# First attention: VectorE's operations in another order, weighing one step later, centring on ScalarE

## The reference, cut to what matters

```
q, k, v = x @ Wq.T + bq, x @ Wk.T + bk, x @ Wv.T + bv      # 16, 8, 8 heads of 16
q, k = rotated by position (cos, sin)
p = (x / max(|x|, 1e-6)) @ R.T           # for q and k, 8 features a head
feats = concat(sin(p), cos(p)) / 4
kv  = einsum('bhsf,bhsd->bsfd', kp, v)   # sums over the heads
out = einsum('bhsf,bsfd->bhsd', qp, kv)
```

## Time and profile before

| | us |
|---|---|
| median of 3 runs | 2040.08 (2039.08 to 2040.45) |
| profiled execution, its own time | 2036.14 |
| its span | 2034.0 |
| busy: PE, DVE, ACT, POOL | 1682.5, 1383.6, 939.3, 672.0 |
| mean granted TensorE clock | 0.923 |

### The profile page before, as it was taken

How to read it: one execution, slowest core, us unless ns; L and a number is a source line. 1 busy time by engine, 2 the same in 40 slices (tenths; PEclk the granted TensorE clock), 3 DMA queues, 4 the chain that set the end, 5 groups by cost and what they waited for, 6 DMA issues and landing times. The chain is left out here.

```text
span 2034.0 us, 35680 instructions
## 1 busy us (share of the span) xinstructions
PE 1682.5 (83%) x10296; PEld 1295.6 (64%) x10296; DVE 1383.6 (68%) x2825; ACT 939.3 (46%) x2201; POOL 672.0 (33%) x850
## 2 busy tenths in 40 slices
PE   2899985709991780799999999996789999979997
PEld 2787774509991560455555555542579999968886
DVE  5688887506665876977777777760467777646776
ACT  0456562304443651066666666664444444433343
POOL 1555530750007824043434334343000000047760
PEclk9799998959995995899999999998899999989999
DMA  6445523723434996333535354422774444466661
GB/s 217 181 141 168 156 47 65 230 91 117 125 113 127 332 355 190 85 105 86 147 85 144 94 129 109 118 68 64 205 216 125 125 126 125 127 212 182 202 181 47
DMA packets 288529, 293.13 MB, mean 144 GB/s; under 512 B 122665, under 2 KB 245034, under 8 KB 286300
## 3 DMA queue, kind: packets, MB, share of 16 engines
q1 hardware_dynamic: 265340, 236.62, 39.6%
q0 software_dynamic: 18432, 50.36, 7.9%
q10 hardware_dynamic: 4608, 4.20, 0.6%
HBM read 144.97 MB, written 141.82 MB: 141 GB/s over the span
## 5 line engine op out<-in xcount | busy, mean ns | idle before, releaser
L1705 ACT ACTIVATE ca_PT<-ca_psS 128x512 f32<-128x512 f32 (+3 forms) x768 | 344.9, 493 | 272.8 <-PE ca_psS L1740 260.4
L1631 DVE TENSOR_REDUCE ca_part<-ca_psM 128x1 f32<-128x512 f32 (+3 forms) x608 | 368.6, 657 | 85.3 <-PE ca_psM L1725 60.5
L1740 PE MATMUL ca_psS<-ca_QS,ca_KS 128*128 128x512 f32 (+3 forms) x768 | 305.7, 408 | 4.2 <-ACT ca_PT L1705 4.1
L1033 POOL DMA_INDIRECT g_y<-ys_scratch,pos x128 | 129.6, 1013 | 441.7 <-POOLq L68 395.0
L1718 PE MATMUL ca_psM<-ca_KS,ca_QS 126*128 126x512 f32 (+3 forms) x768 | 246.5, 364 | 15.6 <-issue 12.8
L1740 PEld LDWEIGHTS ca_psS<-ca_QS,ca_KS 128*128 128x128 f32 x768 | 147.1, 194 | 106.7 <-ACT ca_PT L1705 101.7
L1718 PEld LDWEIGHTS ca_psM<-ca_KS,ca_QS 126*128 126x128 f32 x768 | 141.1, 193 | 37.9 <-DVE ca_part L1631 15.6
L1752 PE MATMUL ca_psO<-ca_PT,ca_VA 128*32 128x512 f32 (+3 forms) x1536 | 160.7, 497 | 1.3 <-POOL ca_PT L1611 1.3
L1609 POOL TENSOR_TENSOR ca_waited<-ca_waited 1x1 f32<-1x1 f32 x128 | 23.4, 183 | 341.7 <-ACT ca_PT L1705 341.7
L626 POOL DMA_INDIRECT xs_scratch<-x_sb,pos x128 | 123.3, 964 | 36.8 <-issue 36.8
L497 PE MATMUL fa_psO<-fa_weighed,ident 128*128 128x256 f32 x512 | 124.0, 398 | 8.1 <-DVE fa_weighed L356 8.0
(11 more groups left out here) (288 smaller groups left out, 4567.2 us busy)
## 6 DMA issues: line engine op xcount, KB each, us to landing
f_xs<-xs_scratch SPq DMA_DIRECT2D x214, 128.0 KB, 2.1
ys_scratch<-f_ys SPq DMA_DIRECT2D x214, 128.0 KB, 1.7
xs_scratch<-fa_blank SPq DMA_DIRECT2D x32, 640.0 KB, 4.1
ca_QS<-qk_scratch SPq DMA_DIRECT2D x32, 512.0 KB, 6.6
ca_KS<-qk_scratch SPq DMA_DIRECT2D x32, 512.0 KB, 8.2
xs_scratch<-fa_blank SPq DMA_DIRECT2D x32, 384.0 KB, 3.4
f_raw<-in_ffn SPq DMA_DIRECT2D x16, 608.0 KB, 4.0
v_scratch<-gp_v_st SPq DMA_DIRECT2D x32, 256.0 KB, 4.5
```

The lines of the kernel that those rows point to most:

```text
L1033: pool.indirect_dma_start(dst[:, k, :], None, y_dram, bass.IndirectOffsetOnAxis(pos[:, tile, k:k + 1], 0)).then_inc(got, 16)
L1631: dve.tensor_reduce(dst, psM[(slot * NU + u) % SLOTS][:, 0:nh * w].rearrange("p (h k) -> p h k", h=nh), AX.X, ALU.max)\
L1705: act.activation(PT[:, s % 2, h, off:CHUNK], psS[(GH * s + h) % SLOTS][:, off:CHUNK], ACT.Exp)\
L1740: pe.matmul(psS[tile % SLOTS][:, off:CHUNK], KS[:, slot, h, kt * P:(kt + 1) * P], QS[:, slot, h, c * CHUNK + off:(c + 1) * CHUNK], start=T ...
```

## The change

VectorE's list is put in another order, with normalise first; the centring moves from VectorE to ScalarE, where it is an activation with a bias of -4 from a new tile; weigh goes from lag 10 to 11, sum_groups from 11 to 12, take_out from 12 to 13, store from 13 to 14. A third memset fills the bias tile, and SP, TensorE and ScalarE wait for it.

```diff
-            in_steps(sp, (0, empty), (1, keep), (13, store), first=16)
+            in_steps(sp, (0, empty), (1, keep), (14, store), first=16)
...
-            def centre(t, i, b):
-                dve.wait_ge(A_done, t + 1)
-                dve.tensor_scalar(A[:, i % 2, :, :], A[:, i % 2, :, :], RF / 2.0, None, ALU.subtract).then_inc(centred, 1)
...
-            in_steps(dve, (1, low_half), (4, bounded_norm), (10, sine_sums), (4, inverse_norm), (0, normalise), (7, in_turns),
-                     (10, centre), (7, whole_turns), (10, weigh), (7, fraction), (2, square_norm), (8, differences), first=16)
+            in_steps(dve, (0, normalise), (1, low_half), (2, square_norm), (11, weigh), (4, bounded_norm), (4, inverse_norm),
+                     (7, in_turns), (7, whole_turns), (7, fraction), (10, sine_sums), (8, differences), first=16)
...
+            def centre(t, i, b):
+                act.wait_ge(A_done, t + 1)
+                act.activation(A[:, i % 2, :, :], A[:, i % 2, :, :], ACT.Identity, bias=minus[:, 0:1]).then_inc(centred, 1)
...
-            in_steps(act, (0, high_half), (1, take_qkv), (9, sines), (1, take_v), (1, keep_logits), (2, keep_rotT), (12, take_out),
-                     (9, squares), (3, keep_p), (3, norm), first=16)
+            act.wait_ge(ones_done, 3)
+            in_steps(act, (11, centre), (0, high_half), (1, take_qkv), (9, sines), (1, take_v), (1, keep_logits), (2, keep_rotT),
+                     (13, take_out), (9, squares), (3, keep_p), (3, norm), first=16)
...
+            pool.memset(minus[:, :], -RF / 2.0).then_inc(ones_done, 1)
...
-            in_steps(pe, (1, project), (0, transpose), (2, transpose_rotated), (11, sum_groups), (3, random_projection), first=16)
+            in_steps(pe, (1, project), (0, transpose), (2, transpose_rotated), (12, sum_groups), (3, random_projection), first=16)
```

More of the change, by code:

```diff
@@ L245, in first_attention @@
         out = sb("out", [P, 2, NQ])
+        minus = sb("minus", [P, 1])
         blank = sb("blank", [P, EMPTY[1] * HID])
@@ L258, in _ @@
         def _(sp):
-            sp.wait_ge(ones_done, 2)
+            sp.wait_ge(ones_done, 3)
             def keep(t, i, b):
@@ L489, in _ @@
             pe.wait_ge(bias_part, 4)
-            pe.wait_ge(ones_done, 2)
+            pe.wait_ge(ones_done, 3)
             def sum_groups(t, i, b):
```

## The result

The changed kernel took 2068.13 us in the median (2060.66 to 2075.55), the kernel before 2040.07; the ratio is 1.014, 95% interval 1.0102 to 1.0177. Run again beside the experiments it took 2063.47 against 2040.3: 1.0101 (1.0058 to 1.0144). Slower, as forecast, but by 23 to 28 us, not 7, and outside the range.

The account below looks back on a forecast made before the run. TensorE and VectorE, both about nine tenths busy, bound the first attention; four groups 5.0, fifth fourth step 0.8, tail 1.0 and last centring 0.1 gave +6.9 us: 2043.0 profiled, 2047.0 on the median's scale, range 2033 to 2056.

Parts of the forecast that it names:

- the stall moves from bounded_norm to weigh: VectorE, every fourth step: idle time sits before weigh, released by ScalarE's centring, some 1.5 to 2.1 us.
- TensorE no longer waits for normalise but for low_half: TensorE: waits for normalise's result are gone, and those for low_half's result are about 4 us each.
- a fourth step is 11.5 us: First attention, every fourth step: centring behind table load and root delays weigh, and low_half's result comes at 11.49 us.
- the others alternate between 7.3 and 7.9: Ordinary steps of the first attention: 7.32 us, then 7.93 when weigh waits for GpSimd's L444, in turn.
- the worked 34.06 us for four steps: Steady part: 11.49 + 7.32 + 7.93 + 7.32 us; 33.9 was taken, +1.25 on the old 32.62.
- the port conflicts between VectorE and GpSimd: Some VectorE instructions and GpSimd's exclude each other; L436 and L444 hold VectorE off 0.9 us, L441 0.5.
- the price of chained instructions: VectorE: in_turns, whole_turns, fraction in a row cost +0.18 us a step; bounded_norm and inverse_norm +0.3 every fourth step.
- Sine_sums never waits: VectorE: sine_sums needs no port and runs beside GpSimd's L436; given as a sign that the forecast is right.
- table loads rival: ScalarE: activation with bias needs loads of 1.28 us each step, about +46 us, 2086; chance 0.02.
- the next begins as the first did: Working of ordinary steps: after the 7.93 us step, the following one starts like the first, of 7.32 us.
- Much slower: Rival: ordinary steps lose 0.6 to 0.8 us to the port, each group gets a clock fall; +14, 2054 us; chance 0.19.
- The tail: End of the stage, GpSimd done, VectorE setting the pace: 8 steps costing 1.0 us, and 0.1 for the last centring.

Follow-up runs that it names:

- with the clock kept up: The changed kernel plus 16 unread 128x128 matmuls at the end of TensorE's step in every fourth step: 2042.76 us, ratio 1.0021 to the kernel before.
- later turns: Kernel before, with bounded_norm and inverse_norm at the end of VectorE's step and in_turns and everything after it one step later: ratio 0.9983, again 0.9964 (2029.66 us).

## Why the prediction was off

**Right.** That the stall moves from bounded_norm to weigh (forecast some 2 us, measured 1.91); that TensorE no longer waits for normalise but for low_half, about 4 us each (3.85); that bounded_norm takes near 1 us (1.00); that a fourth step is 11.5 us (11.35) and the others alternate between 7.3 and 7.9 (7.1 to 8.0 with the clock kept up). With 34.1 against the worked 34.06 us for four steps, the port conflicts between VectorE and GpSimd and the price of chained instructions are right as a sum. Sine_sums never waits in the steady steps. But with the clock kept up the kernel is only 2 us slower than the kernel before, so that the forecast of slower came true owes most to what it left out.

**Smaller misses in it.** Centring takes 0.39 to 0.40 us on ScalarE, not 0.27. The table loads rival is out: there is no load at L419 in the trace, and the other loads number 8 and 7 as before, so this form of activation needs no table beyond those of sine and of root. There the trace agrees with the Trainium skill (ScalarE: Activation LUTs, Table sets: the hidden batching unit), which has identity in every set. The rule of the Trainium skill (VectorE: DVE Perf Modes, The DRAIN you can't avoid) that a semaphore between chained instructions costs nothing extra would, by the prediction's sum, have put the four steps near 33 us; with the clock kept up they take 34.1, on the side of the rows, though no run here took the chain alone away.

**The step that failed** is in the working of the ordinary steps, where the one behind a fourth step was worked like any other ("the next begins as the first did"), with centring on time because TensorE's step was taken as 7.32 us whatever had gone before. From the start of project to the start of random_projection it took 10.5 us in place of 6.7, since TensorE ran that step at a lowered clock after its 3.85 us of waiting. In the sum that gave the forecast, the falls of the clock were a term of nothing. They were priced only in the rivals, at 1.5 us each, as read from the kernel before (where two of the three cost that and the one in a fourth step 0.2); the cost here is (151.1 - 136.4) / 4 = 3.7 a group. In the kernel before the recorded falls in the steady part last 3.4 us each; in the changed one 10.2, 10.2, 6.8 and 10.2. That I took only what a fall had cost in another order, and neither its length nor its place in the step, is the error. The rival Much slower had a fall in each group, at 1.5 us; its other and larger term, 0.6 to 0.8 us lost to GpSimd in every ordinary step, did not come: with the clock kept up these steps are as the forecast had them.

How the place of centring and the clock share the loss can be read from four runs, 16 steps each:

| | clock left to fall | clock kept at 1.00 |
|---|---|---|
| centring behind keep_p and norm | 151.1 (37.4 us lowered) | 136.4 |
| centring ahead of keep_p | 134.1 (17.0 us lowered) | 127.2 |

Either remedy by itself takes most of the loss away: -21 us in the median with the clock kept up, -19 us with the centring moved (2063.47 to 2044.07, in different sets, each some 2 us from its own kernel before); both together end 5 us below the kernel before. But the clock costs something in both rows, 14.7 us and 6.9. Per us of lowered clock that is 0.39 and 0.41, and with the centring on VectorE 9.9 for 23.8 us, 0.42 (139.4 against 129.5); estimates, from one profile of each kernel. So the queue behind keep_p didn't make a slow microsecond dearer: weigh is held up by centring in one case and by sum_groups in the others, at about the same price. What the place of centring did was to add 9.2 us with the clock kept up, and to lengthen TensorE's waits (3.85 us in place of at most 2.1), behind which the clock stayed down for more than twice as long.

**The tail** was forecast at +1.9 us with its last fourth step and took +7.7. With the matmuls it is 65.3 in place of 60.8, so +4.5 remain that aren't the steady part's clock. Once GpSimd is done, steps take 5.62 us against 5.30, +0.3 each where I had 0.13, but the very last ones are shorter than before, so that the last five intervals between sine_sums take 24.5 us in both kernels. The loss lies ahead of them, between the 31st low_half and the 27th sine_sums: 44.1 us against 36.3, and 40.8 with the matmuls. There the clock is lowered for 6.8 us from 295.5 on, and weigh then waits 3.36 us for centring (L353 at 305.23). What the other 4.5 us are made of was not separated.

**Open.** What decides whether the clock falls and for how long. It fell in the kernel before with waits of 1.8 us, in the kernel before with matmuls in that wait, and not in the profiled later turns with waits up to 1.0. Why the steps ahead of the steady ones take 97 us in one execution and 106 in another is open too.

## What to carry to other kernels

An instruction that is moved to an idle engine is late by all that stands ahead of it in that engine's queue, and that includes whatever those wait for: look at what stands in front of it in its slowest step, not at its own length. When a stall is moved, ask also what the engine that now idles does afterwards, for TensorE may come back at a lowered clock, and price the slow step by how long the clock stays down and by whether that time lies in a step that TensorE needs whole. If one cycle of a pipeline stalls for a result made elsewhere, making it a step earlier relative to its use (here, its users a step later) did better than every re-ordering tried without spare matmuls, and as well as the best one with them (0.9964 and 0.9966).

## What the runs showed that was not expected

- Useless matmuls made a kernel 21 us faster (2063.47 to 2042.76), with the granted clock going from 0.88 to 1.00 over the 16 steps and TensorE's recorded busy time the same (134.2 and 134.0 us) though 64 more matmuls (128 in the record) ran in them.
- The same remedy did nothing for the kernel before (1.0011, clock 0.95).
- What a fall of the clock costs goes with its place in the step. In the changed kernel, its variants and the kernel before, a microsecond at the lower clock in ordinary steps cost about 0.4 us; with the gap widened to 4.6 us in the old order the falls lay inside the long fourth step, and 23.8 us of them cost some 4.5.
